# Four small-head attentions of a transformer kernel: keys and values ahead of the first scores, another order on GpSimd, the output projection one period later, the next norm's first half at the end

## The reference

```python
wq = (q @ wq_w.T + wq_b).reshape(b, t, H, DH)
wk = (k @ wk_w.T + wk_b).reshape(b, t, H, DH)
wv = (v @ wv_w.T + wv_b).reshape(b, t, H, DH)
scores = jnp.einsum('bthd,bshd->bhts', wq, wk) / jnp.sqrt(jnp.float32(DH))
probs = jax.nn.softmax(scores, axis=-1)
attn = jnp.einsum('bhts,bshd->bthd', probs, wv)
return attn.reshape(b, t, d) @ wo_w.T + wo_b
```

## Time and profile before

| what | value |
|---|---|
| median of three timed runs | 1412.95 us (1411.89 to 1414.21) |
| the profiled execution | 1408.57 us |
| its span | 1406.8 us |
| busy: PE, PE weight loads, DVE, ACT, POOL | 1154.6, 739.4, 784.7, 656.9, 325.5 us |
| stretch of L0 (135 to 214): PE busy, granted clock | 66.33 of 79 us, 0.96 |
| stretch of L1 (368 to 439) | 58.89 of 71 us, 0.86 |
| stretch of L2 (932 to 995) | 52.20 of 63 us, 0.97 |
| stretch of L3 (1198 to 1278) | 69.09 of 80 us, 0.97 |

### The profile page before, as it was taken

One profiled execution on the slowest core, in us unless ns is written; L12 is line 12 of the kernel. 1 busy time (PEld: TensorE's weight loads), 2 busy tenths in 40 slices (PEclk: granted clock), 3 DMA queues, 4 the chain that ended last, 5 costly groups with the idle time before them and its releaser, 6 DMA issues. The chain is left out here.

```text
span 1406.8 us, 25020 instructions
## 1 busy us (share of the span) xinstructions
PE 1154.6 (82%) x9528; PEld 739.4 (53%) x9528; DVE 784.7 (56%) x1966; ACT 656.9 (47%) x1370; POOL 325.5 (23%) x321
## 2 busy tenths in 40 slices
PE   6997885569698996678886983988889988898998
PEld 4565453337365663336744752856434444455776
DVE  3565436567565447887787788356361555452111
ACT  2564333441244225586677673444566442334332
POOL 1333100013211003754446450140000034300000
PEclk9999997566798998797997996699899999999999
DMA  7000000200000000000000000043095700000000
GB/s 294 1 2 1 1 2 1 92 1 1 0 3 1 1 0 1 0 1 2 1 1 2 1 1 1 2 195 141 5 209 118 156 1 2 1 2 2 1 1 16
DMA packets 15207, 44.39 MB, mean 32 GB/s; under 512 B 1873, under 2 KB 4977, under 8 KB 14449
## 3 DMA queue, kind: packets, MB, share of 16 engines
q1 hardware_dynamic: 15088, 42.80, 10.4%
HBM read 42.01 MB, written 0.79 MB: 30 GB/s over the span
## 5 line engine op out<-in xcount | busy, mean ns | idle before, releaser
L842 ACT ACTIVATE L_xattn_pT<-banks 128x512 f32<-128x512 f32 x128 | 69.2, 602 | 107.1 <-PE banks L739 107.1
L239 POOL TENSOR_TENSOR norm_rstd<-norm_var,norm_power 128x4 f32<-128x4 f32 x24 | 24.5, 1024 | 362.3 <-DVE norm_var L232 362.2
L887 DVE TENSOR_REDUCE L_xattn_top<-banks 128x4 f32<-128x512 f32 x128 | 79.5, 684 | 44.1 <-PE banks L712 44.1
L1469 DVE TENSOR_TENSOR L_ffn_a<-L_ffn_a,L_ffn_share 128x512 f32<-128x512 f32 x64 | 39.9, 685 | 60.3 <-DMA L_ffn_share<-L_ffn_shares 57.6
L1383 PE MATMUL banks<-L_ffn_a,region_a 128*128 128x512 f32 x136 | 67.5, 601 | 5.0 <-DVE L_ffn_a L1469 5.0
L1702 ACT ACTIVATE L_ffn_aT<-banks,L_ffn_shift 128x512 f32<-128x512 f32 x64 | 43.3, 687 | 58.9 <-PE banks L1654 57.3
L1374 PE MATMUL banks<-hT,region_a 128*128 128x512 f32 x136 | 68.5, 609 | 0.0
L1715 DVE SCALAR_TENSOR_TENSOR x<-banks,L_ffn_combine,x 128x128 f32<-128x128 f32 x64 | 18.0, 344 | 88.7 <-PE banks L1665 88.7
L1665 PEld LDWEIGHTS banks<-region_b,L_ffn_aT 128*128 128x128 f32 x512 | 59.5, 192 | 6.7 <-issue 6.7
L1538 PE MATMUL banks<-hT,region_a 128*128 128x512 f32 x128 | 60.4, 617 | 1.3 <-PEq L78 1.3
L488 ACT ACTIVATE L_attn_p<-banks,L_attn_shift 128x129 f32<-128x129 f32 x128 | 45.4, 368 | 34.4 <-DVE L_attn_shift L538 34.4
(11 more groups left out here) (521 smaller groups left out, 2934.9 us busy)
## 6 DMA issues: line engine op xcount, KB each, us to landing
L_ffn_share<-L_ffn_shares SPq DMA_DIRECT2D x32, 512.0 KB, 10.6
region_b<-in_L_ffn SPq DMA_DIRECT2D x1, 6216.0 KB, 29.7
region_a<-in_L_ffn SPq DMA_DIRECT2D x1, 4416.0 KB, 13.7
region_b<-in_L_attn SPq DMA_DIRECT2D x1, 3150.5 KB, 12.2
region_a<-in_L_ffn SPq DMA_DIRECT2D x1, 3080.5 KB, 21.8
region_b<-in_L_attn SPq DMA_DIRECT2D x1, 1633.5 KB, 9.6
region_b<-in_L_xattn SPq DMA_DIRECT2D x1, 835.0 KB, 10.3
w_tables<-in_tables SPq DMA_DIRECT2D x1, 832.0 KB, 13.3
```

Source lines behind the costliest of these rows:

```text
L842: nc.scalar.activation(pT[:, n % 2, 4 * i:4 * i + 4, :], rows_of(flip[i][:], 4), ACT.Exp, scale=scale).then_inc(exped, 1)
L887: nc.vector.tensor_reduce(top[:, 32 * i:32 * i + 32:HD], rows_of(score[i][:], 4), X, ALU.max).then_inc(topped, 1)
L1469: nc.vector.tensor_tensor(a[:, k % AHEAD, :], a[:, k % AHEAD, :], share[:, batch % RING, j, :], ALU.mult).then_inc(weighed, 1)
```

## The change

It touches this function alone, and keeps what it computes.
- All keys and values are made ahead of the first scores (in L0, whose second keys need the second half of the norm, the values alone). The first scores no longer wait for the values to be kept; three of the banks change places.
- Where the first half of `hT` is there (L0 and L2, `split`), the first keys are made in two pieces of 256 tokens, and VectorE spreads the second piece, ahead of the norm's moments.
- GpSimd takes the powers of the norm ahead of its memsets of `values`.
- `project` and the addition to x come one period later, ScalarE copies `raw` ahead of `oT`, TensorE turns the maxima ahead of the output, and the waits that the banks need are added (the last projections wait for `added`).
- The next norm's first half: moments at the start of k = 8, scaling at k = 9, transposes at k = 10.

```diff
-    LAST = B + 3
+    LAST = B + 4
+    split = Norm.is_kept(g)
+    FIRST = HALF // 2 if split else HALF
...
-    hT_bank, q_bank, k_bank, v_bank = (bank[0], bank[4]), (bank[2], bank[5]), (bank[1], bank[6]), (bank[3], bank[7])
+    hT_bank, q_bank, k_bank, v_bank = (bank[0], bank[4]), (bank[2], bank[7]), (bank[1], bank[6]), (bank[7], bank[5])
...
+            norm.invert(pool, 0)
+            nc.gpsimd.memset(top[:], 0.0)
+            nc.gpsimd.tensor_scalar(minus[:], bc(g.in_group[:], 2, T), -1.0, None, ALU.mult).then_inc(minus_ready, 1)
+            norm.invert(pool, 1)
             for b in range(4):
                 nc.gpsimd.memset(values[:, b, :, :], 0.0)
-            nc.gpsimd.memset(top[:], 0.0)
-            nc.gpsimd.tensor_scalar(minus[:], bc(g.in_group[:], 2, T), -1.0, None, ALU.mult).then_inc(minus_ready, 1)
             pool.drain()
             nc.gpsimd.memset(counters[:, 0:32, :], 1.0).then_inc(cleared, 1)
-            norm.invert(pool, 0)
-            norm.invert(pool, 1)
...
+            def make_first_keys():
+                nc.tensor.matmul(k_bank[0][:, 0:FIRST], w["wk"], keys_from[:, 0:FIRST], start=True, stop=True).then_inc(k_made, 1)
+                if split:
+                    nc.tensor.matmul(k_bank_too[:, 0:HALF - FIRST], w["wk"], keys_from[:, FIRST:HALF],
+                                     start=True, stop=True).then_inc(k_made_too, 1)
+
+            def make_more_keys():
+                nc.tensor.matmul(k_bank[1][:], w["wk"], half_of(keys_from, 1), start=True, stop=True).then_inc(k_made, 1)
...
                 if n == 0:
                     pe.wait_ge(q_kept, 1)
                     pe.wait_ge(k_kept, 4)
-                    pe.wait_ge(v_kept, 1)
+                if n == 0 and split:
+                    pe.wait_ge(k_kept_by_dve, 4)
...
             def project(n):
                 pe.wait_ge(oT_kept, n + 1)
-                if n + 2 < B:
-                    pe.wait_ge(exped, G * (n + 2) + 2)
+                if n + 3 < B:
+                    pe.wait_ge(exped, G * (n + 3) + 2)
+                if n >= 1:
+                    pe.wait_ge(added, n)
...
             if norm.kept:
                 make_queries(0)
+                make_first_keys()
+            elif keys_here:
+                norm.turn(pe, 0, hT_bank[0])
+                make_queries(0)
+                make_first_keys()
+            else:
+                make_first_keys()
+            make_values(0)
             if not keys_here:
-                make_keys(0)
-            if norm.scaled and not norm.kept:
+                make_more_keys()
+            make_values(1)
+            if not norm.kept and not keys_here:
                 norm.turn(pe, 0, hT_bank[0])
-            make_values(0)
...
             scores(0)
             norm.turn(pe, 1, hT_bank[1])
             make_queries(1)
-            make_keys(1)
-            make_values(1)
+            if keys_here:
+                make_more_keys()
             turn_top(0)
...
+                if k < B:
+                    turn_top(k)
                 if 0 <= k - 3 < B:
                     turn_out(k - 3)
-                if k < B:
-                    turn_top(k)
-                if 0 <= k - 3 < B and out_weight is not None:
-                    project(k - 3)
+                if carries and k == B + 2:
+                    ahead.turn(pe, 0, score[2])
+                if 0 <= k - 4 < B and out_weight is not None:
+                    project(k - 4)
                 if 0 <= k - 2 < B:
                     turn_mixed(k - 2)
-                if carries and k == B:
-                    ahead.turn(pe, 0, score[2])
...
+            keep_values(0)
             if not keys_here:
-                keep_keys()
...
+                keep_more_keys()
+            keep_values(1)
             norm.keep(act, 1, hT_bank[1])
             keep_queries(1)
-            act.wait_ge(k_made, 2)
-            nc.scalar.activation(kT[:], k_bank[1][:], ACT.Identity, bias=w["bk"]).then_inc(kT_kept, 1)
-            keep_values(1)
+            if keys_here:
+                keep_more_keys()
             for k in range(1, LAST):
                 if 0 <= k - 1 < B:
                     weigh(k - 1, (0, 1))
+                if 0 <= k - 2 < B:
+                    keep_raw(k - 2)
                 if 0 <= k - 3 < B:
                     keep_out(k - 3)
-                if 0 <= k - 2 < B:
-                    keep_raw(k - 2)
...
+            def keep_keys():
+                dve.wait_ge(shift_ready, 1)
+                dve.wait_ge(k_made_too, 1)
+                for r in range(4):
+                    nc.vector.tensor_scalar(ks[:, r, FIRST:HALF], k_bank_too[:, 0:HALF - FIRST], g.in_group[:, r:r + 1], shift[:, r:r + 1],
+                                            ALU.mult, ALU.add).then_inc(k_kept_by_dve, 1)
...
+            if split:
+                keep_keys()
             norm.take_moments(dve, 0)
             norm.take_moments(dve, 1)
...
+                if carries and k == 8:
+                    dve.drain()
+                    ahead.take_moments(dve, 0)
+                if carries and k == 9:
+                    norm.await_turned(dve, 1)
+                    ahead.scale(dve, 0)
                 if k < B:
                     find_top(k)
                     keep_top(k)
-                if 0 <= k - 3 < B and out_weight is not None:
-                    add(k - 3)
+                if 0 <= k - 4 < B and out_weight is not None:
+                    add(k - 4)
                 if 0 <= k - 2 < B:
                     normalise(k - 2)
-                if carries and k == 7:
-                    dve.drain()
-                    ahead.take_moments(dve, 0)
-                if carries and k == 8:
-                    norm.await_turned(dve, 1)
-                    ahead.scale(dve, 0)
```

47 lines of the change are left out of this document (28 added, 19 removed).

## The result

The changed kernel takes 1390.18 us (median of 4, 1387.83 to 1395.57), the kernel before 1413.58 beside it (median of 4, 1411.89 to 1418.02): a ratio of 0.9833 with a 95% interval of 0.981 to 0.9856, 23.4 us faster. 1390.18 lies 0.8 us under the low end of the predicted range, and 8.4 us under the predicted 1398.6.

What follows compares the result with a forecast made beforehand. Bound: a loop ring beside TensorE's issue time, waits for ScalarE's copies, and stage heads and tails. Gains 7.2 (loop) + 3.0 (tails) + 4.2 (heads) = 14.4 off 1408.57 give 1394.2, plus 4.4 offset 1398.6 us; range 1391 to 1408.

Steps and rivals of the forecast that it cites:

- The loop, 7.2: Loops of all four stages: turn_mixed comes 0.36 us sooner in five periods each, period 4.98 us, 7.2 us gained.
- The rival that the ring keeps the loop long: Loop: the ring turn_mixed, reciprocal, `o`, flip (or the exps) replaces the gap, 7.2 us not gained, 1406 us; chance 0.12.
- The tails, 3.0: Tails of the four stages: last mixture starts sooner; 0.7 us gained in L2 and L1, 1.0 L3, 0.6 L0.
- the transposes now lie in that chain, +1.1: L2's tail, from last mix to end: the next norm's four transposes add 1.1 us to that chain.
- L1 alike 0.7: L1's tail: the same gain as in L2's tail, 0.7 us.
- L1's head, 4.7: L1's head: clock rises and stays, second scores 4.4 us behind the first, at 383.75 against 388.48; 4.7 us gained.
- L3's head, 0.4: L3's head: second scores at 1214.5 against 1214.91, 0.4 us gained; bounds -1 and 2.
- L0's head, 1.2: L0's head: chain ends at about 150.3 at full clock, 152.3 at low, against 153.54; 1.2 us gained taken.
- L2's head, -2.1: L2's head: VectorE's keys delay moments, power, memsets, second values and `hT`; second scores later, 2.1 us lost taken.
- the upper bound of 3.5: L2's head: if the clock falls, low-clock queries and scores cost 2 us more, 3.5 us lost.
- the carried offset: Whole kernel: median of timed runs 4.4 us above the profiled execution before, carried over to the forecast.
- The rival "more gained": Other stages find better places of the clock and L1's tail does not slow: 20 us gained, 1393 us; chance 0.09.

Runs made afterwards that it cites:

- e1_old_head: The changed kernel's loop and tail with the head of the kernel before: 1397.47 us, ratio 0.9881 to the kernel before.
- e5_warm: The changed kernel plus three unused TensorE products in the head pauses of L0 and L2: 1384.6 us, ratio 0.9808 to the kernel before.
- e3_old_ahead: The changed kernel with the next norm's first half left where it was before: 1394.38 us, ratio 0.9862 to the kernel before.
- e9_before_warm: The kernel before plus unused TensorE products in the pauses of L1's stage, no order changed: 1410.97 us, ratio 0.9976 to the kernel before.
- e2_new_head: The changed kernel's head with the loop and tail of the kernel before: 1407.72 us, ratio 0.9944 to the kernel before.
- e7_old_pool: The changed kernel with GpSimd's queue order of before: 1389.93 us, ratio 0.9824 to the kernel before.
- e8_again: The changed kernel unaltered, measured again in another session: 1392.41 us, ratio 0.9853 to the kernel before.
- e11_before_third: The kernel before, unaltered, run again for a third profile: 1409.82 us.
- e4_moments_first: The changed kernel, but VectorE takes the norm's moments ahead of its share of the keys: 1379.86 us, ratio 0.976 to the kernel before.

## Why the prediction was right in kind and short in size

By the profiles of before and after, in the order of the prediction's sum (14.4 predicted, 18.2 measured in the four stages):

- **The loop, 7.2.** Right in place and nearly in size: 1.79, 1.94 and 1.82 us in L0, L1 and L3 against 1.8 each, the period 4.94 against 4.98, no wait ahead of `project`. L2's loop gives -0.74, mostly as the low clock reaches into its first periods; at full clock it gives 1.5 (`e1_old_head`) or 1.7 (`e5_warm`). The rival that the ring keeps the loop long is out.
- **The tails, 3.0: the step that failed.** Measured 0.63, 3.45, 1.33 and 1.67, in all 7.1. The mechanism is right, two sizes are not. First "the transposes now lie in that chain, +1.1": I took the 1.10 us of the earlier trace rows for their cost, but in those rows each waits for its own scaling; with `h` long ready they hold the queue for 0.44. That is 0.66 in each of L1 to L3, 2.0 in all, and by just that L2's tail is shorter than predicted (9.73, not 10.4). `e3_old_ahead` measures the place at 0.86 a stage, where 1.6 - 1.1 = 0.5 was in the sum. Second, "L1 alike 0.7": L1's tail of before ran partly at the low clock, 14.10 us where L2's took 11.99. `e9_before_warm` brings it to 12.00, so 2.1 of its 3.45 are the clock.
- **L1's head, 4.7.** Measured 6.0 (20.44 to 14.45), and 7.4 against the mean of the three profiles of before. The second scores stand 4.49 behind the first, as said; the first came at 9.96 instead of 11.3, since the clock rose sooner in this execution (11.49 and 11.41 in `e2_new_head` and `e7_old_pool` with the same queue on TensorE). The Trainium skill, page "TensorE: Matmul & The Clock Gate", Part 1, has the throttled state as the default that activity releases; `e9_before_warm` and `e5_warm` agree, where added work alone turns 0.58 into 1.00 and 0.50 into 1.00.
- **L3's head, 0.4**: 1.1. **L0's head, 1.2**: 0.26 in one profile and -0.2 in the other, against the first profile of before; against the three of before (15.80 to 18.70, mean 17.3) it is a loss of 1.1 and 1.6. Whether that head gained at all is not shown.
- **L2's head, -2.1.** Second scores 1.07 later, and 1.7 more lost in the first scores and flips at the low clock: 2.8, between the 2.1 that I took and the upper bound of 3.5. The chain was read rightly, memsets, second values and `hT` included, and ran 1.4 us sooner than I had it (memsets done 10.95 into the stage, 12.4 predicted); that four scalings would take 4.14 us beside the memsets no row of mine held, and `e8_again` shows that it cost nothing. The other 0.7 that the loop lost is a pause at the full clock, which no term had.
- **The rest, and the carried offset.** 2.6 us of the profiles' 20.8 lie in stages that nothing touches, whose sum differs by 10 us between the profiles here; the runs do not settle whether a part of it belongs to the change (the 4.6 us of the delta-rule attention, under `e8_again`). The offset from profiled execution to median was 4.4, as carried over; here it is 2.4.

The miss of 8.4 us (1398.6 to 1390.2) is so made up: 3.8 in the touched stages, 2.6 in the others, 2.0 of offset. The 3.8 are tails +4.1, L1's and L3's heads +2.0, L0's head -0.9, L2's head and loop -1.5 (1.8 lost where 0.3 was due), the other loops +0.1. The 2.6 and the 2.0 come from no term of the sum and could have had the other sign. Of the 3.8, `e8_again` shows 1.0 (15.4 against 14.4), the rest of it being 1.7 in L0's dense layers and 1.1 in the heads and L2's loop; the tails are the same there within 0.02 us, so their +4.1 is the part that stands (+3.1 if L1's tail of before is taken from `e11_before_third`, 13.15). That the first median fell 0.8 us outside the range and the second 1.4 inside is luck; that the tails' term was too small is not. The rival "more gained" held what happened, L1's tail at the full clock and 20 us. Its chance of 0.09 looks too small: the clock is worth 5.5 us in L1's stage, and the stretches shown before the prediction had that stage at 0.86 where the three others had 0.96 or 0.97. I priced the clock in L1's head and left out its tail.

## What to carry to other kernels

Price a moved instruction by what it holds in the queue once its inputs are ready, not by the length of a row in which it waits piece by piece. Read the granted clock of every head and tail before the sum: in L1 a change that filled TensorE's pauses was worth its order (7.0 us) plus the clock behind them (5.5), and in L2 one that opened a pause paid both; a few unused products in the pause show which. Profile the kernel before more than once where its clock moves: the same head of it came out 3 us apart in three profiles. When an engine is given a new duty at a stage's head, put it behind the work that another engine's chain waits for: the same four instructions ahead of the moments or behind them differ by 10 to 13 us here.

## What the runs showed of the hardware

- VectorE's four scalings of 128 x 128 float32 took 1.11 us alone. Where GpSimd's memsets had begun 0.56 or 0.93 us before them they took 1.20 and 1.27 (`e4_moments_first`). Where the memsets had begun 0.08 or 0.09 us before them they took 1.66, 2.12, 2.49, 2.73 or 4.14, and different values came out in different executions of one kernel (1.66 and 2.49 in L2's head of the kernel before, 4.14 and 2.12 in that of the changed one). With a product of 3.63 us among them they took 5.77. The Trainium skill, page "SBUF — State Buffer", section "🔬 SBUF: two separate sides", describes a port that VectorE and GpSimd hold in turn, one shutting the other out. The 5.77, with a last scaling that ends with GpSimd's product, agrees; the 1.20 and 1.27 show next to nothing of it, and what decides between 1.66 and 4.14 was not tested.
- The clock falls and rises at other places of the same kernel from run to run, where TensorE has pauses: the second scores of L1 came at 20.44, 21.97 and 23.17 in the kernel before. The price in L1's stage is 5.5 us of 72; the loops of that kernel repeat within 0.15 us.
- In L2's loop, just as the loads of the next weights end, TensorE shows pauses at the full clock that no semaphore explains. One row of the changed kernel, and one of `e4_moments_first`:

```profile
943.31 0.71 PE L757 MATMUL banks<-L_xattn_topT,L_xattn_minus 32*128 32x128 f32 x12 [0.83 <-issue]
```

```profile
940.46 1.06 PE L770 MATMUL banks<-L_xattn_pT,L_xattn_values 128*32 128x128 f32 x27 [1.38 <-issue]
```

The DMA share is 0.89 in 940 to 942 and 0.13 in 942 to 944 of the former, and 0.98, 0.15 and 0.00 in the three stretches of 2 us from 935 to 941 of the latter, so the pauses lie behind the loads and not beside them. The interval between flips that holds the pause is 6.14 us in the changed kernel and 6.60 in `e4_moments_first`, where the loop has 4.94 otherwise, but `e7_old_pool` has none above 5.09. The cause was not tested, and stays open.
